# Near products in two terms, ten extra products ahead of two waits, and a later token scatter

## The chip, the cores and the metric

The kernel runs on one core of a Trainium2 chip. The metric is the time of one execution on the device in microseconds; the kernel before takes 2100.75 us, the median of 3 runs (2097.2 to 2100.86).

## The reference, cut to what matters

A transformer block on 16 sequences of 512 tokens with 256 features, in float32:

```python
qkv = x @ Wqkv + bqkv                       # 16 heads of 16 features
scores = stack([(q * shift(k, d)).sum(-1) for d in OFFSETS]) * scale + pos_bias   # d = 0..32, 48, 64, 96, 128, 192, 256, 384
alpha = softmax(scores)                     # over the 39 offsets, -inf where d > position
out = sum(alpha[d] * shift(v, d) for d in OFFSETS)
x = layernorm(x + (out * sigmoid(x @ Wgate + bgate)) @ Wout + bout)
logits = relu(x @ rw1 + rb1) @ rw2 + rb2    # 8 experts, the best 2 of each token, at most 1024 tokens an expert
x = layernorm(x + experts(x))               # relu(x @ ew1 + eb1) @ ew2 + eb2, weighted by the softmax of the two logits
```

## The kernel before

The kernel has three stages behind a short setup: `attention` (everything up to the first normalization, the router and the dispatch of tokens), `experts` and `combine`. The change touches `attention` alone. Float32 values are carried as a float16 high part plus a float16 low part, and a product is made of three terms, high by high, high by low and low by high.

`attention` works on one sequence (a batch) at a time, in a software pipeline. `run_iterations` writes the same plan for each engine: 20 iterations (-2 to 17), each of 16 slots; the middle ones, 2 to 13, are a hardware loop over two iterations at a time. `SLOTS_OF` (line 54) says which parts stand in which slot, `AHEAD` which batch a stage works on (the maxima on the next one, the output product on the one before, the ranking and the scatter on the one before that), and `LATER` by how many slots an engine takes a part later than TensorE (1 if it isn't named). Each engine takes its work strictly in that order. The tables `SCORES_AT`, `EXP_AT`, `SPLIT_AT`, `VALUES_AT` and `EVAC_AT` (lines 76 to 80) put the attention pairs into slots in the same way: a batch has 6 pairs k, 2 far ones (offsets that are multiples of 16) and 4 near ones (offsets 0 to 32, one for each tile of 128 tokens). A pair goes through `scores` (TensorE, banks `st`, lines 563 to 590), `weights` (ScalarE: the exponential twice, as float16 at line 789 and as float32 at line 790), `split_weights` (line 394: the float32 minus the float16, one half on VectorE and one on GpSimd), `values` (TensorE, line 622, banks `o[0]` and `o[1]`), and then either `evacuate_far` (ScalarE) or `merge` (VectorE, line 897: the near result plus the far one that came back through DRAM as `o_back`).

In `values` a near pair uses one `o` bank, `o[k % 2]`; for each of 4 blocks, 4 groups and 2 halves e it does three matmuls: high weights by the high values with the ones column (2 x 17 columns), high weights by low values (2 x 16), low weights by high values (2 x 17). All three add up in the same 17 columns.

The parts that matter beside these, in TensorE's order within an iteration: slot 5 `outp t` (transposes of the gated output, line 539), slot 6 `outp w` (its product with `wout`, line 546) and `maxp near0` (lines 678 to 688, which a reduction on VectorE, line 952, follows), slots 7 and 8 `near1` to `near3`, slots 9 and 10 `far0`, `far1` (lines 698 and 706), slot 10 `rout t`, slots 11 to 14 the router's hidden layer (`rout h0` to `h3`, line 546), slot 15 `feat x` (transposes of a new x), slots 0 and 1 the q and k projections. These parts share three PSUM banks `gp` in turn; by that order `outp w`'s first unit has the same bank as `outp t`'s first. ScalarE copies the transposed halves to `featT` (line 804). `rank s0` to `s3` issue on GpSimd two indirect DMAs each (line 1093), which scatter a batch's rows to their experts in DRAM (`disp`).

## Time and profile before

| | |
|---|---|
| median of 3 runs | 2100.75 us |
| the profiled execution | 2102.96 us |
| its span in the trace | 2101.2 us, mean granted TensorE clock 0.784 |
| busy in the span | TensorE 74%, VectorE 46%, ScalarE 43%, GpSimd 32% |
| costliest on TensorE | line 546 with `wr` 193.2 us, line 1385 173.0, line 1399 170.1, line 622 near 317 in all |

The attention stage fills about the first 1670 us, the experts run up to about 2055, and the rest is the last normalization. In the profile PE is TensorE, PEld its weight loads, DVE is VectorE, ACT ScalarE, POOL GpSimd, SP the queue that issues most DMAs. A bracket behind a row gives the idle time just before it and what ended that; "issue" there means that nothing the profile shows was waited for.

### The profile page before, as it was taken

Reading aid. Unit: us, or ns where it says so; the run is one execution under the profiler, and the core shown is the slowest. Engines: PE = TensorE matmul, PEld = TensorE weight load, DVE = VectorE, ACT = ScalarE, POOL = GpSimd, SP = SyncE. Lnnn points to the kernel's source line nnn. Section 1 sums busy time; section 2 is a strip of 40 time slices with the busy share of each in tenths; the row PEclk is TensorE's granted clock in tenths of the full one; section 3 lists DMA queues with packets and bytes.
Section 4 is the critical chain, followed back from the end, with each engine's and each line's share of the span. In section 5 each row is a group of like instructions: output and inputs, shape, how many; then the busy total and the mean of one; then the engine's idle time right before and its main releaser. Section 6 shows DMA issues by size and latency. Waiting matters only on the chain. (4 is left out here: it accounts for less than half of the span.)

```text
span 2101.2 us, 76212 instructions
## 1 busy us (share of the span) xinstructions
PE 1556.9 (74%) x33280; PEld 1045.3 (50%) x33280; DVE 962.6 (46%) x1925; ACT 907.8 (43%) x1544; POOL 674.4 (32%) x654
## 2 busy tenths in 40 slices
PE   0455786878777787878787777869676389999980
PEld 0234555545454455545455554545454247667660
DVE  4213354544445444545454454445455255554535
ACT  1232353534443352635254433526343366565626
POOL 4221333323241423333233415243332303232335
PEclk9665787868776786868687767768687689999995
DMA  3374524525251524334252514243330144444328
GB/s 82 63 203 135 107 77 92 103 76 114 74 117 49 114 64 96 82 74 98 63 114 64 115 49 103 64 87 74 66 86 3 45 134 102 98 90 111 66 31 325
DMA packets 220118, 194.80 MB, mean 93 GB/s; under 512 B 66847, under 2 KB 207151, under 8 KB 219648
## 3 DMA queue, kind: packets, MB, share of 16 engines
q1 hardware_dynamic: 204464, 175.11, 33.7%
q0 software_dynamic: 15360, 15.10, 4.5%
q8 instruction: 266, 4.36, 0.9%
q14 instruction: 28, 0.23, 0.0%
HBM read 98.07 MB, written 86.18 MB: 88 GB/s over the span
## 5 line engine op out<-in xcount | busy, mean ns | idle before, releaser
L394 POOL TENSOR_TENSOR p<-p 128x512 f16<-128x512 f32 x96 | 135.9, 1416 | 522.4 <-ACT p L790 522.2
L804 ACT COPY featT<-gp 128x1024 f16<-128x1024 f16 x96 | 93.4, 1032 | 430.4 <-PE gp L539 430.4
L394 DVE TENSOR_TENSOR p<-p 128x512 f16<-128x512 f32 x96 | 86.4, 900 | 293.4 <-ACT p L790 293.0
L546 PE MATMUL gp<-featT,wr 128*128 128x512 f16 x768 | 193.2, 410 | 19.8 <-DVE mT L945 13.6
L622 PE MATMUL o<-v_near,p 128*32 128x34 f16 (+1 forms) x6144 | 161.2, 185 | 33.9 <-issue 31.4
L1385 PE MATMUL up<-rowsT,w 128*128 128x512 f16 x768 | 173.0, 386 | 9.7 <-DVE w L1462 5.3
L622 PEld LDWEIGHTS o<-v_near,p 128*32 128x32 f16 x6144 | 153.7, 98 | 51.0 <-issue 47.9
L1347 POOL DMA_INDIRECT xln<-y,place x64 | 104.8, 1637 | 220.0 <-DVE y L1489 179.4
L789 ACT ACTIVATE p<-st 128x512 f16<-128x512 f32 x192 | 116.7, 608 | 126.1 <-PE st L590 109.4
L1399 PE MATMUL dn<-w,h 128*128 128x256 f16 x1536 | 170.1, 273 | 0.0
L1093 POOL DMA_INDIRECT disp<-y,sidx x128 | 137.9, 1078 | 65.2 <-issue 49.2
L1399 PEld LDWEIGHTS dn<-w,h 128*128 128x128 f16 x1536 | 149.7, 98 | 17.3
L952 DVE TENSOR_REDUCE m_near<-gp 128x8 f16<-128x512 f32 x128 | 82.1, 682 | 146.7 <-PE gp L688 93.8
L1446 ACT ACTIVATE h<-up,b 128x512 f16<-128x512 f32 x128 | 88.2, 689 | 131.1 <-PE up L1385 73.1
L546 PEld LDWEIGHTS gp<-featT,wr 128*128 128x128 f16 x768 | 76.0, 104 | 120.6 <-issue 35.3
L1385 PEld LDWEIGHTS up<-rowsT,w 128*128 128x128 f16 x768 | 76.0, 99 | 100.9 <-issue 11.4
L1080 POOL TENSOR_TENSOR x<-xin,x 128x1024 f16<-128x1024 f32 x16 | 34.0, 2125 | 280.2 <-ACT x L811 280.2
L1501 DVE TENSOR_TENSOR h<-h 128x512 f16<-128x512 f32 x128 | 88.6, 693 | 70.7 <-ACT h L1447 70.6
L546 PE MATMUL gp<-wout,featT 128*128 128x256 f16 x384 | 81.4, 405 | 49.8 <-ACT featT L804 49.8
L790 ACT ACTIVATE p<-st 128x512 f32<-128x512 f32 x192 | 118.1, 615 | 0.0
L546 PE MATMUL gp<-featT,wqk 128*128 128x512 f16 x384 | 112.9, 465 | 1.4 <-ACT featT L804 1.2
L874 ACT ACTIVATE hid<-gp,br 128x512 f16<-128x512 f32 x128 | 88.6, 692 | 55.6 <-PE gp L546 51.9
(173 smaller groups left out, 2953.7 us busy)
## 6 DMA issues: line engine op xcount, KB each, us to landing
qk_dram<-qk SPq DMA_DIRECT2D x64, 256.0 KB, 2.5
v_near<-vs SPq DMA_DIRECT2D x224, 66.0 KB
qs<-qk_dram SPq DMA_DIRECT2D x96, 128.0 KB, 4.6
ks<-qk_dram SPq DMA_DIRECT2D x96, 128.0 KB, 7.7
o_dram<-o_far SPq DMA_DIRECT2D x64, 136.0 KB, 5.9
o_back<-o_dram SPq DMA_DIRECT2D x16, 544.0 KB
v_dram<-vs SPq DMA_DIRECT2D x16, 528.0 KB, 3.3
v_far<-v_dram SPq DMA_DIRECT2D x64, 132.0 KB, 3.5
```

The source lines that it names most:

```text
L394: engine.tensor_tensor(p16[:, b, 1, :], p32[:, b, :], p16[:, b, 0, :], ALU.subtract).then_inc(is_split, 1)
L546: last = nc.tensor.matmul(dst, lhs(a, c), rhs(b, c), start=(k == 0), stop=(k == len(todo) - 1))
L622: last = nc.tensor.matmul(dst[quad, :, 2 * z + e, 0:cols.stop - cols.start], p16[:, 2 * (k % 2) + e, a, c:c + BLOCK], v[:, :, 2 * z + e, c ...
L789: nc.scalar.activation(p16[:, b, 0, :], bank[:, :], ACT.Exp)
L790: nc.scalar.activation(p32[:, b, :], bank[:, :], ACT.Exp).then_inc(exp_ready, 1)
L804: gp_done(nc.scalar.copy(featT[:, i, :, :].rearrange("f c t -> f (c t)"), bank[:, :].bitcast(F16)), n, stage, PART_OF_T[stage], i)
L874: nc.scalar.activation(hid16[:, 0, ht, :], bank[:, :], ACT.Relu, bias=br1[:, ht:ht + 1], scale=1.0 / WS)
L1093: nc.gpsimd.indirect_dma_start(out=disp[:, :], out_offset=bass.IndirectOffsetOnAxis(ap=sidx[:, t, k:k + 1], axis=0), in_=y16[n.par][:, t, ...
L1347: nc.gpsimd.indirect_dma_start(out=xln[:, :], out_offset=bass.IndirectOffsetOnAxis(ap=place[:, gr, t:t + 1], axis=0), in_=y[:, gr, t, :], ...
L1385: last = nc.tensor.matmul(up[h % 4][:, :], w1[e.par][:, a, c, P * h:P * (h + 1)], rowsT[:, gr, b, c, :], start=(k == 0), stop=(k == 5))
L1399: last = nc.tensor.matmul(dn[u][:, D * (t % 2):D * (t % 2 + 1)], h16[:, gr, a, h, P * t:P * (t + 1)], w2[e.par][:, b, h, :], start=(k == 0 ...
L1501: nc.vector.tensor_tensor(h16[:, gr, 1, h, :], h32[:, h % 2, :], h16[:, gr, 0, h, :], ALU.subtract).then_inc(h_lo, 1)
```

## The change

It has four parts. `rank s0, s1` move from slot 6 to slot 11 and `rank s2, s3` from slot 7 to slot 13 (GpSimd takes each one slot later). A near pair's three terms become two matmuls: high weights by high and low values together (2 x 33 columns), and low weights by high values (2 x 17) added onto the first 17; the results of the halves e go to the banks `o[0]` and `o[1]`, so that each near pair takes both and waits for the merge of the pair before. `merge` adds `o_back` to the first 17 columns of both halves and then, after a wait on its own semaphore, the other 16: four operations for one. And `keep_warm` writes ten 512-column products of router weights, which are overwritten by what follows, into the bank that the next part uses: ahead of the gated product in `outp w`, and ahead of the second far scores.

```diff
-    6: [("outp", "w"), ("maxp", "near0"), ("rank", "s0"), ("rank", "s1")],
-    7: [("rank", "s2"), ("rank", "s3"), ("outp", "y"), ("maxp", "near1")], 8: [("maxp", "near2"), ("maxp", "near3")],
+    6: [("outp", "w"), ("maxp", "near0")],
+    7: [("outp", "y"), ("maxp", "near1")], 8: [("maxp", "near2"), ("maxp", "near3")],
...
-    11: [("maxp", "t"), ("rout", "h0")],
-    12: [("rout", "h1"), ("gate0", "den0"), ("gate0", "inv0")], 13: [("rout", "h2")], 14: [("rout", "h3")], 15: [("feat", "x")],
+    11: [("maxp", "t"), ("rout", "h0"), ("rank", "s0"), ("rank", "s1")],
+    12: [("rout", "h1"), ("gate0", "den0"), ("gate0", "inv0")], 13: [("rout", "h2"), ("rank", "s2"), ("rank", "s3")], 14: [("rout", "h3")], 15: [("feat", "x")],
...
+            def keep_warm(bank, count):
+
+                for _ in range(count):
+                    nc.tensor.matmul(bank[:, :], wr1[:, 0, 0, 0:P], wr1[:, 0, 0, 0:512], start=True, stop=True)
...
+                banks = [st[(2 * k + e) % ST_BANKS] for e in range(2)]
+                if k == 1:
+                    wait(alone, exp_ready, n.at(2 * UNIT_PAIRS, 2 * k + 1 - ST_BANKS))
+                    keep_warm(banks[0], 10)
                 wait(alone, exp_ready, n.at(2 * UNIT_PAIRS, 2 * k + 2 - ST_BANKS))
...
-                elif k <= FAR_PAIRS + 1:
-                    alone.wait_ge(far_out, n.at(FAR_PAIRS, min(k, FAR_PAIRS)))
+                elif k <= FAR_PAIRS:
+                    alone.wait_ge(far_out, n.at(FAR_PAIRS, k))
                 else:
-                    alone.wait_ge(merged, n.at(TILES, k - FAR_PAIRS - 1))
+                    alone.wait_ge(merged, n.at(TILES, k - FAR_PAIRS))
...
+                            if not far:
+                                v = v_near[:, 4 * (k - FAR_PAIRS) + blk, :, 2 * z + e, :]
+                                dst = o[e][:, 0:PAIRS * VW].rearrange("q (u z c) -> q u z c", u=2, c=VW)[quad, :, z, :]
+                                nc.tensor.matmul(dst, p(0), v, start=True, stop=False, skip_group_check=True)
+                                last = nc.tensor.matmul(dst[:, :, 0:OW], p(1), v[:, :, 0:OW], start=False, stop=True, skip_group_check=True)
+                                continue
...
-                    drained(pe, n, "outp", "t", 0)
-                    drained(pe, n, "outp", "t", 1)
                     for u in range(2):
                         bank, is_full = unit(n, "outp", "w", u)
+                        if u == 0:
+                            keep_warm(bank, 10)
+                            drained(pe, n, "outp", "t", 0)
+                            drained(pe, n, "outp", "t", 1)
...
-                nc.vector.tensor_tensor(ob[:, i, :, :].rearrange("q h c -> q (h c)"), o[i % 2][:, 0:H * OW],
-                                        o_back[:, i, :, :].rearrange("q h c -> q (h c)"), ALU.add).then_inc(merged, 1)
+                of_e = lambda t, e: t[:, i, :, :].rearrange("q (u z e) c -> q e u z c", u=2, e=2)[:, e]
+                src = [o[e][:, 0:PAIRS * VW].rearrange("q (u z c) -> q u z c", u=2, c=VW) for e in range(2)]
+                for e in range(2):
+                    last = nc.vector.tensor_tensor(of_e(ob, e), src[e][:, :, :, 0:OW], of_e(o_back, e), ALU.add)
+                last.then_inc(merge_hi, 1)
+                dve.wait_ge(merge_hi, n.at(TILES, i + 1))
+                for e in range(2):
+                    num = of_e(ob, e)[:, :, :, 0:HD]
+                    last = nc.vector.tensor_tensor(num, src[e][:, :, :, OW:VW], num, ALU.add)
+                last.then_inc(merged, 1)
```

## Rows read from the trace of the kernel before

**Rows 1.** The page: busy time by engine, then TensorE's granted clock in 40 slices
```profile
PE 1556.9 (74%) x33280; PEld 1045.3 (50%) x33280; DVE 962.6 (46%) x1925; ACT 907.8 (43%) x1544; POOL 674.4 (32%) x654
...
PEclk9665787868776786868687767768687689999995
```

**Rows 2.** Timeline, TensorE, line 681: start us, us, instructions [idle before]; three of 16 batches
```profile
239.58 0.48 PE L681 MATMUL gp<-near_bias,sel_first 32*128 32x512 f16 x2
...
329.15 0.38 PE L681 MATMUL gp<-near_bias,sel_first 32*128 32x512 f16 x2
...
1482.93 0.38 PE L681 MATMUL gp<-near_bias,sel_first 32*128 32x512 f16 x2
```

**Rows 3.** Operations by tile, `disp`, GpSimd: ns min/median/max, first and last start us
```profile
L1093 POOL DMA_INDIRECT disp<-y,sidx x128: 966/976/2010, 335.2 to 1669.2; - x128
```

**Rows 4.** Timeline, TensorE, from near1 to far0 in an iteration with a scatter
```profile
719.85 0.39 PE L678 MATMUL gp<-near_bias,sel 32*128 32x512 f16 x2
...
723.70 0.27 PE L688 MATMUL gp<-ks,qs 16*32 16x64 f16 x5 [0.46 <-issue]
...
733.07 0.61 PE L678 MATMUL gp<-near_bias,sel 32*128 32x512 f16 x2 [3.64 <-DVE m_near L952]
...
735.23 0.39 PE L698 MATMUL gp<-far_bias,sel 32*128 32x256 f16 x2 [0.88 <-DVE m_near L952]
```

**Rows 5.** Timeline, TensorE, near1 and far0 in iteration 1, which has no scatter
```profile
245.13 0.39 PE L678 MATMUL gp<-near_bias,sel 32*128 32x512 f16 x2
...
254.41 0.40 PE L698 MATMUL gp<-far_bias,sel 32*128 32x256 f16 x2 [0.90 <-DVE m_near L952]
```

**Rows 6.** Timeline, GpSimd, first and last of the scatter's eight DMAs
```profile
720.24 1.11 POOL L1093 DMA_INDIRECT disp<-y,sidx  x1 [0.91 <-issue]
...
730.10 0.98 POOL L1093 DMA_INDIRECT disp<-y,sidx  x1 [0.30 <-issue]
```

**Rows 7.** Timeline, VectorE: two reductions of near2, and the merge of pair 4
```profile
732.23 1.29 DVE L952 TENSOR_REDUCE m_near<-gp 128x8 f16<-128x512 f32 x2 [6.32 <-remote]
...
761.17 0.43 DVE L897 TENSOR_TENSOR ob<-o,o_back 128x272 f32<-128x272 f32 x1
```

**Rows 8.** Timeline, GpSimd, its subtractions for pairs 4 and 5
```profile
752.15 1.61 POOL L394 TENSOR_TENSOR p<-p 128x512 f16<-128x512 f32 x1
761.68 1.54 POOL L394 TENSOR_TENSOR p<-p 128x512 f16<-128x512 f32 x1 [7.92 <-ACT p L790]
```

**Rows 9.** Timeline, TensorE, the parts that the change touches or meets in this iteration
```profile
708.94 5.30 PE L546 MATMUL gp<-wout,featT 128*128 128x256 f16 x24 [3.32 <-ACT featT L804]
...
749.05 4.08 PE L546 MATMUL gp<-featT,wr 128*128 128x512 f16 x12 [0.26 <-issue]
...
760.45 5.35 PE L546 MATMUL gp<-featT,wr 128*128 128x512 f16 x24
765.73 2.33 PE L622 MATMUL o<-v_near,p 128*32 128x34 f16 x96
...
775.59 0.40 PE L563 MATMUL st<-sel,far_bias 64*128 64x256 f16 x2 [2.25 <-ACT p L790]
...
783.72 2.54 PE L622 MATMUL o<-v_far,p 128*32 128x68 f16 x96
```

**Rows 10.** Timeline, TensorE, wide products of the expert stage
```profile
1856.59 10.52 PE L1385 MATMUL up<-rowsT,w 128*128 128x512 f16 x48
```

**Rows 11.** Timeline, GpSimd, the indirect DMA beside them
```profile
1859.63 1.56 POOL L1347 DMA_INDIRECT xln<-y,place  x1 [11.45 <-DVE y L1489]
```

**Rows 12.** Timeline, ScalarE, its copies of the transposed gated output
```profile
706.91 1.98 ACT L804 COPY featT<-gp 128x1024 f16<-128x1024 f16 x2
```

**Rows 13.** Stretches: from:to us, length, busy by engine (instructions), granted TensorE clock, DMA share, GB/s
```profile
708.90:714.20 5.30, 5.26 (x26) 3.40 (x28) 3.20 (x13) 0.00 (x0) 1.14 (x1) 0.50 0.76 148
...
732.00:751.00 19.00, 15.26 (x527) 11.21 (x528) 5.67 (x10) 3.98 (x6) 1.18 (x2) 0.59 0.02 3
...
775.50:779.00 3.50, 3.41 (x135) 2.13 (x136) 3.46 (x3) 0.94 (x2) 1.20 (x1) 0.50 0.43 94
```

## What the change will do to the time

> **What bounds the kernel now.** I read the shares of busy time on the page first: TensorE is busy for 74% of the span, no other engine for half of it [rows 1]. The 40 slices then show where its clock is held back: in the attention loop, slices 2 to 31, it is granted at 5 to 8 tenths, while the expert stage behind it has 9s [rows 1]. So the loop over 16 batches is TensorE's: its instructions stand in one order for all batches, and what it waits for, or does at half clock, is time. How long one batch takes is read from the first near-maximum product (line 681), which stands once in each iteration: between the iterations that start it at 329.15 and at 1482.93 lie twelve, 96.15 us each; but the iteration from 239.58 to 329.15 took 89.57 us [rows 2]. The two differ in the one thing that the diff moves: the first scatter of tokens (line 1093) comes at 335.2 [rows 3], so iteration 1 has none, and iterations 2 to 14 have one beside the near-maximum products.
>
> The timeline of TensorE shows what it does there. With a scatter, the products from near1 on (719.85) reach far0 at 735.23, 15.4 us later; without one the same work goes from 245.13 to 254.41, 9.3 us [rows 4, 5]. Inside the scatter (GpSimd's row at 720.24; its last DMA at 730.10) [rows 6] TensorE issues three to five products and stands 0.46 us, with no releaser but "issue" [rows 4], and it then waits 3.64 us for VectorE's reduction [rows 4], which itself had stood 6.32 us for something the profile calls "remote" [rows 7]. Neither is there in iteration 1. The chain of what ended last is no help for this: it lies in the last normalization.
>
> **The change part by part.** The profiled execution took 2102.96 us, its span 2101.2 with 1.8 around it, and the median of three runs is 2100.75. I make the sum against 2102.96 and take the 2.2 off at the end.
>
> *The scatter moves* from GpSimd's places at slots 7 and 8 to slots 12 and 14 of an iteration: eight indirect DMAs, the last starting 9.86 us after the first [rows 6], so 1.4 from one to the next; four and four make two stretches of 5.2. What it gives back is 15.4 - 9.3 = 6.1 us by the stretch, 96.15 - 89.57 = 6.6 by the whole iteration. 13 iterations by 6.3 make **-82 us** (-79 to -86). With the gaps gone, what is late next in the stretch is the chain through VectorE, GpSimd and ScalarE that makes y, and the wait for each reduction; both are inside the 9.3 already.
>
> What it costs in its new place: GpSimd reaches slot 12 after its subtraction for pair 4 (752.15, 1.61 long) and slot 14 after pair 5 (761.68, 1.54) [rows 8]. The four DMAs would run from about 753.8 to 758.9 and from 763.2 to 768.4. GpSimd has nothing due between (its next subtraction is that of the first far pair, whose exponential TensorE itself still waits for at 775.59 [rows 9], by when GpSimd is free), and the semaphores that the scatter waits for are long up. Its buffers are wanted again in the next iteration's slot 6, over 35 us later. TensorE does wide products there: the second stretch lies beside line 546 (760.45, 24 of them) and then the 96 products of pair 5 (765.73) [rows 9]. In the expert stage an indirect DMA of 1.56 us at 1859.63, with three behind it, leaves the 48 wide products from 1856.59 on whole: 10.52 us, 0.219 each, no gap [rows 10, 11]. So wide products aren't held. Narrow ones are, three to five in 0.73 us (the row's 0.27 and the 0.46 ahead of it) [rows 4]: pair 5 would overlap the second stretch by at most 2.7 us. SP's queue issues the maxima, the copies of v and the next x beside these stretches; none is wanted before the next first far scores. Below: 0. Above: the whole 6.6 comes back. I take 1.5 a batch, near the lower end because that is the case of the expert row and the stretch is cut in two, over 14 iterations: **+21 us**.
>
> That TensorE should suffer at all is against the Trainium skill: "SBUF — State Buffer", section "Who interferes with whom", says that only the port pair shared by VectorE and GpSimd contends and that TensorE and ScalarE wait for nobody. By that rule the 0.46 us gaps are none of the scatter's and would stay; the case is the first rival below, and the trace with and without a scatter speaks against it.
>
> *The near product of values (line 622)* goes from three matmuls of 34, 32 and 34 columns to two of 66 and 34: 96 a pair become 64, with as many weight loads. 96 near ones take 2.33 us, 24.3 ns each; 96 far ones, of 68 and 64 columns, take 2.54, so 26.5 each [rows 9]. Doubling the columns costs 2 ns: it is their number that counts. 64 take 32 x 26.5 + 32 x 24.3 ns = 1.63 us, a gain of 0.70. Pairs 3, 4 and 5 of a batch lie in TensorE's dense stretches (3 x 16 x 0.70 = 34 us); pair 2 lies ahead of near1, whose reduction waits for y anyway, and counts a quarter: **-37 us**. Bounds: 0, were it the columns that count (they stay 100), and -45 with pair 2 in full.
>
> *The merges on VectorE (line 897)*: one addition of 272 elements, 0.43 us [rows 7], becomes two of 136, a wait for their end, and two of 128. A reduction of 512 elements takes 0.65 (two in 1.29) [rows 7], so an element costs 0.9 ns and an operation 0.2 beside that: 528 elements in four operations are 1.3 us, +0.85 each, and each result now uses both o banks, so that pair k waits for the merge of k - 1 and not of k - 2. The tightest is pair 5: merge 4 begins at 761.17 and would end at 762.5, pair 5 starts at 765.73 [rows 7, 9]. In VectorE's queue behind a merge stand the hidden layer's subtractions, which ScalarE needs three products later. 0 us; if the cover is gone (VectorE held by the scatter), 0.85 x 16 = 14.
>
> *Ten products ahead of the gated product.* They go into bank 0, which the first gated transpose also used, so they start only when ScalarE's first copy is done: two copies, 1.98 us from 706.91 [rows 12], hence 707.9. The old wait ended at 708.94, so just 1.0 of its 3.32 us is left to fill. A 512-column product takes 0.219 at full clock [rows 10], about twice that at half: ten end between 710.1 and 712.2. What they could give is the clock: the 24 products after the wait took 5.3 us [rows 9] at a granted clock of 0.50 [rows 13] and would take half that at full clock. Old end 714.2; new end between 710.1 + 2.65 = 712.8 and 712.2 + 5.3 = 717.5. The clock fell with an idle stretch of 3.3 us and 2.3 of these stay, so it still falls; it may rise sooner. I take the middle, +1.0 a batch.
>
> *Ten ahead of the second far scores*: TensorE ended its transposes at 773.34 and waited 2.25 us for ScalarE [rows 9]. The products fill that at full clock (2.19) and overshoot by 2 at half. The 3.5 us after the wait were at 0.50 [rows 13], worth 1.7. Between -1.8 and +2.0; middle -0.6, since a fuller stretch brings the clock back sooner and the wait is nearly as long as they are. Both together (1.0 - 0.6) x 16 = **+6 us**, bounds -51 and +85, each only if all 32 fall to one side.
>
> **Sum**: -82 + 21 - 37 + 6 = -92. 2102.96 - 92 = 2011; less 2.2, **2009 us**.
>
> **Rivals.** *The gaps belong to the narrow products, not to the scatter*: then moving it gives nothing and costs nothing, -37 + 6 = -31, **2070 us**. For it: the gaps sit only on narrow products. Against: iteration 1 has these and not the gaps [rows 5]. 8%. The Trainium skill's rule named above is this case.
>
> *The clock comes back in the near stage.* Granted was 0.59 from 732 to 751, with the narrow products dense for much of it [rows 13]. If the shorter stage lets it rise earlier, the transposes and the first hidden product (749.05, 12 in 4.08 us, where 24 of them take 5.35 later) [rows 9] save about 2.6 us a batch: 34 more, **1975 us**. Against: iteration 1's stage has VectorE's waits too. 10%.
>
> *The hold moves along, and gets worse (slower).* VectorE's reduction at 732.23 started 12.0 us after the scatter's first DMA [rows 6, 7]. If each half holds VectorE in slots 12 to 15, the merge of pair 4 comes late, pair 5 must wait for it (a wait that the change adds), the subtractions keep ScalarE from draining, and the wide products run out of banks. At 4 us of holding twice and 3.6 of narrow products in pair 5 and the next far scores, 11.6 a batch: 14 x 11.6 = 162 in place of 21, with the rest -113: **2150 us**. It decides from (82 + 37 - 6)/14 = 8.1 us a batch on. For it: the remote wait has no named cause [rows 7]. Against: each half is half as long and meets wide products. 7%.
>
> *The products cost at half clock throughout*: +85 in place of +6, the rest holding: **2088 us**. Against: 24 wide products at 760.45 took 5.35 us [rows 9], full speed, so the clock does return under dense work. 5%.
>
> **Numbers.** Forecast 70%, gaps stay 8, clock back 10, hold moves 7, half clock 5. The range must leave out 2 in 10 at most: from 1975 (clock back) to 2072, which takes in the case that the gaps stay and most of the upper end of the new place (6.6 a batch, 2009 + 71 = 2080). Faster by over 0.2% 0.89, within 0.2% 0.03, slower 0.08; 0.2%, 4 us, is about what a measurement of this kernel can tell.
>
> **What would show it.** Right: line 681's starts 90 us apart in all iterations; no 0.46 us gaps from near1 to far0; 4096 near matmuls in 64s of 1.6 us; gated product starting 1 to 3 us later after its wait, scores' transposes followed by ten products and no wait. Wrong: gaps still in near1 (first rival); VectorE waiting for "remote" after slot 12, or "values" waiting for line 897's successors (third). The step I trust least is the price of the scatter's new place, then the clock after the ten products.

## The result: 30 us faster, a third of what was forecast

The changed kernel takes 2071.01 us (median of 4 runs, 2067.58 to 2081.45), the kernel before 2100.81 beside it (4 runs, 2097.2 to 2103.67): ratio 0.9867, 95% interval 0.9829 to 0.9906. Forecast was 2009. The profiled execution took 2071.61 us with a span of 2069.9 and a mean granted TensorE clock of 0.827 (0.784 before). The first busy line and the clock line of its page, which answer to [rows 1]:

```profile
PE 1571.6 (76%) x31552; PEld 1021.9 (49%) x31552; DVE 992.3 (48%) x2117; ACT 905.3 (44%) x1544; POOL 703.0 (34%) x654
...
PEclk9676788879787887979787887978787699999995
```

TensorE is busy 15 us longer (320 extra products, less the shorter near ones) and its clock line has more 8s and 9s in the attention loop; the span still lost only 31 us. Line 693 is the old line 681; its starts, as in [rows 2]:

```profile
327.17 0.38 PE L693 MATMUL gp<-near_bias,sel_first 32*128 32x512 f16 x2
...
1450.06 0.38 PE L693 MATMUL gp<-near_bias,sel_first 32*128 32x512 f16 x2
```

Twelve iterations take 93.57 us each, against 96.15. I use this measure for all kernels below ("an iteration"): the start of the fourth such product to that of the sixteenth, by 12. It is read from the one profiled execution of each kernel.

**What went as forecast.** The stretch of [rows 4], from near1 to far0 (lines 690 and 710 now), in the changed kernel, and then the group of the near-maximum products over the whole run, before and after (operation, count, ns min/median/max; under it the idle time before them, us and times):

```profile
707.67 0.39 PE L690 MATMUL gp<-near_bias,sel 32*128 32x512 f16 x2
...
709.06 0.61 PE L700 MATMUL gp<-ks,qs 16*32 16x64 f16 x56 [0.85 <-issue]
712.93 0.61 PE L690 MATMUL gp<-near_bias,sel 32*128 32x512 f16 x2 [3.25 <-DVE m_near L974]
...
717.76 0.39 PE L710 MATMUL gp<-far_bias,sel 32*128 32x256 f16 x2 [0.88 <-DVE m_near L974]
```

```profile
L688 PE MATMUL gp<-ks,qs x4096: 171/227/238, 85.4 to 1502.3; 16*32 16x64 f16 x185, 16*32 16x32 f16 x11
...
  issue: 148.7, 260
```

```profile
L700 PE MATMUL gp<-ks,qs x4096: 171/226/238, 83.6 to 1464.0; 16*32 16x64 f16 x185, 16*32 16x32 f16 x11
...
  issue: 39.7, 81
```

near1 starts at 707.67, far0 at 717.76: 10.1 us, against 15.4. The products still stand once for 0.85 us, not every few products, and over the run their "issue" time fell from 148.7 us in 260 places to 39.7 in 81. So the gaps left with the scatter, and VectorE's waits for "remote" too (its waits over the run: us, times, longest), before and after:

```profile
DVE m_near L952 <- remote: 53.0, 9, 8.4
```

```profile
DVE ob L914 <- remote: 8.3, 2, 4.2
```

**What did not.** In the gated product's place (TensorE's timeline and two stretches; columns as in [rows 13]):

```profile
695.29 4.45 PE L545 MATMUL gp<-wr 128*128 128x512 f16 x10 [2.40 <-ACT featT L818]
699.53 3.17 PE L551 MATMUL gp<-wout,featT 128*128 128x256 f16 x24
```

```profile
695.30:699.70 4.40, 4.40 (x11) 1.64 (x12) 3.37 (x12) 0.85 (x1) 2.00 (x1) 0.50 1.15 127
699.80:702.60 2.80, 2.80 (x24) 2.26 (x22) 0.69 (x1) 0.00 (x0) 0.00 (x0) 0.91 0.90 212
```

The ten products run at 0.50 of the clock and take 4.45 us; the 24 behind them then run at 0.91 and take 3.17 instead of 5.30 [rows 9]. Over the run, ten by sixteen each:

```profile
L545 PE MATMUL st<-wr x160: 376/380/634, 110.0 to 1509.4; 128*128 128x512 f16 x160
...
L545 PE MATMUL gp<-wr x160: 379/634/634, 234.9 to 1593.6; 128*128 128x512 f16 x160
```

The median of the ones ahead of the gated product (`gp`) is 634 ns, that of the ones ahead of the second far scores (`st`) 380: the first mostly meet half clock, the second mostly full.

In the scatter's new place (GpSimd, VectorE, TensorE in the same iteration):

```profile
736.01 4.17 POOL L1115 DMA_INDIRECT disp<-y,sidx  x1 [0.17 <-issue]
```

```profile
737.12 1.48 DVE L1006 TENSOR_TENSOR hid<-rows,hid 128x512 f16<-128x512 f32 x2
738.52 0.67 DVE L952 SCALAR_TENSOR_TENSOR og<-eg,ob 128x512 f32<-128x512 f32 x1
```

```profile
737.54 4.45 PE L551 MATMUL gp<-featT,wr 128*128 128x512 f16 x12 [2.07 <-DVE mT L967]
...
743.95 0.19 PE L629 MATMUL o<-v_near,p 128*32 128x66 f16 x1 [0.50 <-issue]
...
744.93 0.18 PE L630 MATMUL o<-v_near,p 128*32 128x34 f16 x1 [0.73 <-issue]
```

The first DMA takes 4.17 us instead of 1.1, TensorE's second hidden product waits 2.07 us for VectorE and takes 4.45 us, and the value products of pair 4 behind it stand several times (0.50, 0.73), so that they reach from 742 to 745.4.

### The profile page after: what moved, and what is told of

Read it like the earlier page. It is cut to its first block and busy times, and to the rows that moved or that the text cites. A ratio compares the mean times of both kernels' runs of the same rounds, so it can differ in the third digit from the quotient of the medians.

```text
span 2069.9 us, 72972 instructions
## 1 busy us (share of the span) xinstructions
PE 1571.6 (76%) x31552; PEld 1021.9 (49%) x31552; DVE 992.3 (48%) x2117; ACT 905.3 (44%) x1544; POOL 703.0 (34%) x654
## 5 line engine op out<-in xcount | busy, mean ns | idle before, releaser
L394 POOL TENSOR_TENSOR p<-p 128x512 f16<-128x512 f32 x96 | 129.6, 1350 | 465.7 <-ACT p L804 465.7
L394 DVE TENSOR_TENSOR p<-p 128x512 f16<-128x512 f32 x96 | 94.9, 988 | 310.6 <-ACT p L804 303.5
L551 PE MATMUL gp<-featT,wr 128*128 128x512 f16 x768 | 204.5, 426 | 26.7 <-DVE mT L967 19.5
L1115 POOL DMA_INDIRECT disp<-y,sidx x128 | 172.6, 1349 | 52.9 <-issue 37.9
L629 PE MATMUL o<-v_near,p 128*32 128x66 f16 x2048 | 132.3, 202 | 43.4 <-issue 31.6
L629 PEld LDWEIGHTS o<-v_near,p 128*32 128x32 f16 x2048 | 118.0, 105 | 67.4 <-issue 66.7
L630 PE MATMUL o<-v_near,p 128*32 128x34 f16 x2048 | 130.8, 192 | 12.5 <-issue 12.4
L630 PEld LDWEIGHTS o<-v_near,p 128*32 128x32 f16 x2048 | 118.5, 98 | 9.9 <-issue 9.3
L867 ACT ACTIVATE y<-y,nmr,rstd 128x256 f32<-128x256 f32 x64 | 33.2, 588 | 180.4 <-POOL nmr L1098 180.4
```

The lines of the kernel that those rows point to most:

```text
L394: engine.tensor_tensor(p16[:, b, 1, :], p32[:, b, :], p16[:, b, 0, :], ALU.subtract).then_inc(is_split, 1)
L551: last = nc.tensor.matmul(dst, lhs(a, c), rhs(b, c), start=(k == 0), stop=(k == len(todo) - 1))
L629: nc.tensor.matmul(dst, p(0), v, start=True, stop=False, skip_group_check=True)
L630: last = nc.tensor.matmul(dst[:, :, 0:OW], p(1), v[:, :, 0:OW], start=False, stop=True, skip_group_check=True)
L1115: nc.gpsimd.indirect_dma_start(out=disp[:, :], out_offset=bass.IndirectOffsetOnAxis(ap=sidx[:, t, k:k + 1], axis=0), in_=y16[n.par][:, t, ...
```

## The experiments

Kernels with the same number for the kernel before ran on one chip, beside it. There turned out to be two sorts of chip: the result and e1 to e8 stand on chips where the kernel before takes about 2100 us (the first sort), e9 to e18 on three others where it takes about 2024 (the second sort). No chip was measured on two occasions, so whether it is the chip itself or something else about the occasion isn't shown; "sort of chip" stands for either.

| kernel | kernel before beside it | median | ratio (95%) | iteration |
|---|---|---|---|---|
| before / the change (result) | 2100.81 | 2071.01 | 0.9867 (0.9829 to 0.9906) | 96.15 / 93.57 |
| e1 no products | 2109.29 | 2030.10 | 0.9628 (0.9581 to 0.9675) | 91.05 |
| e2 no far products | 2109.29 | 2066.34 | 0.9814 (0.9767 to 0.9861) | 92.71 |
| e3 no gated products | 2109.29 | 2047.71 | 0.9716 (0.9670 to 0.9762) | 92.15 |
| e4 scatter moved alone | 2109.29 | 2076.60 | 0.9863 (0.9816 to 0.9910) | 93.62 |
| e5 terms alone | 2096.78 | 2061.49 | 0.9816 (0.9786 to 0.9845) | 93.32 |
| e6 no scatter | 2096.78 | 1966.72 | 0.9368 (0.9336 to 0.9400) | 87.36 |
| e7 far products before branch | 2096.78 | 2045.33 | 0.9733 (0.9691 to 0.9776) | 91.81 |
| e8 first half in q and k | 2096.78 | 2025.72 | 0.9655 (0.9626 to 0.9684) | 90.23 |
| e9 scatter in one place | 2022.41 | 1984.18 | 0.9804 (0.9780 to 0.9828) | 87.64 |
| e10 plain DMAs | 2022.41 | 1976.62 | 0.9767 (0.9736 to 0.9798) | 87.03 |
| e11 four gated products | 2022.41 | 1990.41 | 0.9828 (0.9795 to 0.9862) | 88.51 |
| e12 one part a slot | 2022.41 | 1977.60 | 0.9768 (0.9750 to 0.9787) | 87.33 |
| e13 before again | 2026.19 | 2028.34 | 1.0006 (0.9983 to 1.0029) | 90.23 |
| e14 change again | 2026.19 | 2023.55 | 0.9995 (0.9972 to 1.0018) | 91.08 |
| e15 no products again | 2026.19 | 1976.65 | 0.9768 (0.9727 to 0.9808) | 87.09 |
| e16 one part a slot again | 2026.19 | 1978.17 | 0.9778 (0.9738 to 0.9818) | 87.04 |
| e17 plain DMAs again | 2023.91 | 1981.77 | 0.9805 (0.9771 to 0.9838) | 87.35 |
| e18 one place again | 2023.91 | 1983.89 | 0.9812 (0.9782 to 0.9842) | 87.36 |

### The parts one by one: e1 to e4

e1 is the change without both sets of ten, e2 keeps the gated ones, e3 the far ones, e4 is the kernel before with nothing but the new places of the scatter:

```diff
 # e1 and e2
-                if k == 1:
-                    wait(alone, exp_ready, n.at(2 * UNIT_PAIRS, 2 * k + 1 - ST_BANKS))
-                    keep_warm(banks[0], 10)
 # e1 and e3
-                            keep_warm(bank, 10)
 # e4, in the kernel before
-    6: [("outp", "w"), ("maxp", "near0"), ("rank", "s0"), ("rank", "s1")],
-    7: [("rank", "s2"), ("rank", "s3"), ("outp", "y"), ("maxp", "near1")],
+    6: [("outp", "w"), ("maxp", "near0")],
+    7: [("outp", "y"), ("maxp", "near1")],
...
+    11: [("maxp", "t"), ("rout", "h0"), ("rank", "s0"), ("rank", "s1")],
...
+    13: [("rout", "h2"), ("rank", "s2"), ("rank", "s3")],
```

> The change without its twenty products an iteration; the terms, the merge and the moved scatter stay. From the two traces I read, start to start and as means over iterations 4 to 13: the stretch from the transposes of x to the values of the first far pair grew by 1.4 us, that from the ranking's product to the end of the gated product by 0.6. Theory (they cost more than the clock returns): taking them away gives 2.0 x 15 = 30 us back, 2071 - 30 = 2041. Rival (the prediction's sizes, +1.0 and -0.6 an iteration): 2071 - 6 = 2065, no difference to speak of.

> The change without the ten products ahead of the second far scores, those ahead of the gated product stay. Theory (TensorE's sequencer spends 4.6 us in the loop's branch in every second iteration, and only then comes to the ten products, which therefore fill nothing): 2071 - 1.4 x 15 = 2050. Rival of the prediction (they gain 0.6 an iteration): 2071 + 9 = 2080. The branch's row should fall back from 4.6 us to near the 3.9 of before or stay, and the following wait should again be one for ScalarE's exponential.

> The change without the ten products ahead of the gated product, those ahead of the second far scores stay. Theory: 2071 - 0.6 x 15 = 2062. By the prediction's +1.0: 2056. Were the products worth their price here: 2071 or more. The gated product's 24 matmuls, 3.2 us in the change, should take 5.3 again.

> The kernel before with the scatter moved and nothing else. Theory (the move gives 5.7 us an iteration in the near stage and takes 4.7 in the hidden layer): 13 x 5.7 - 14 x 4.7 = 8 us, 2093. The prediction (82 given, 21 taken): 2040. Rival (the held place is worse without the shorter near products): over 2101.

**Measured**: without any product 2030.1 us, with the gated ones 2066.3, with the far ones 2047.7. By the ratios both together cost 0.9867 - 0.9628 = 0.0239, some 50 us, where the sum had 6 (the intervals of two such ratios leave about 13 us either way); the gated ones alone 36 us (2066.3 - 2030.1), the far ones 18. The moved scatter alone gives 0.0137, 29 us. What I expected of these runs was off in size each time: 30 us for both sets; 21 for taking the far ones out of the change (measured 0.9867 - 0.9814, 11 us) and 9 for taking the gated ones out (0.9867 - 0.9716, 32 us); and 8 for the moved scatter.

Where the far products' time goes is in TensorE's timeline of the change: first an iteration that ends in the hardware loop's branch, then one that doesn't:

```profile
660.63 1.07 PE L539 MATMUL gp<-ident,x 128*128 128x128 f16 x16
665.88 4.13 PE L545 MATMUL st<-wr 128*128 128x512 f16 x10 [4.18 <-ACT p L804]
```

```profile
755.34 1.57 PE L539 MATMUL gp<-ident,x 128*128 128x128 f16 x13
...
757.64 2.67 PE L545 MATMUL st<-wr 128*128 128x512 f16 x10
```

In the second the ten start at once behind the transposes and take 2.67 us, near the 2.19 of the forecast. In the first, TensorE stands 4.18 us before them and they then take 4.13 us. The profile puts the wait down to ScalarE, but in this iteration the branch instruction runs from 660.87 to 665.62, and the ten start at 665.88. The branch (line 189, ns min/median/max), before and after:

```profile
L189 PEldq COMPARE_BRANCH  x6: 82/3858/4057, 481.1 to 1446.8; - x6
```

```profile
L189 PEldq COMPARE_BRANCH  x6: 83/4566/5042, 473.6 to 1413.5; - x6
```

Before, the 3.86 us of the branch lay almost wholly under the wait for ScalarE's exponential: from the transposes of x to the scores behind them it took 4.2 to 4.5 us with a branch and 3.7 to 4.0 without. The change's products stand behind the branch in the order, so in these iterations they don't fill the wait but follow it: 8.8 to 9.7 us with a branch, 4.7 to 6.8 without. The Trainium skill says of this, in "Runtime: NRT & Kernel Launch", section "Instruction fetch mechanics", that a taken branch whose target isn't among the pages at hand forces a fetch before execution goes on, and that straight code mostly hides its fetches; it gives no time. The rows give 3.9 to 4.6 us for the whole branch and don't show what it waits for. With one set alone it stays at 3.4 to 4.1 us (e2, e3), so the 4.6 belongs to both sets together.

### Terms, scatter, and the products ahead of the branch: e5 to e8

e5 is the change with the scatter in its old place and no products. e6 is e1 with the scatter's DMAs and the waits on them left out. e7 is e3 with the ten far products at the end of slot 15. e8 is e1 with the scatter's first half in slot 1 of the next iteration (and the hardware loop from iteration 4 on):

```diff
 # e6
-                        nc.gpsimd.indirect_dma_start(
-                            out=disp[:, :], ...).then_inc(scattered, 16)
 # e7, behind the transposes of x at the end of slot 15
+                m = n.shift(-1)
+                if m.in_range():
+                    wait(alone, exp_ready, m.at(2 * UNIT_PAIRS))
+                    keep_warm(st[2], 10)
 # e8
-    11: [("maxp", "t"), ("rout", "h0"), ("rank", "s0"), ("rank", "s1")],
+    11: [("maxp", "t"), ("rout", "h0")],
+    0: [("scat", "s0"), ("scat", "s1"), ("proj", "qk0"), ("gate", "den1"), ("gate", "inv1")],
```

> The kernel before with the near products in two terms and the four-part merge, scatter in its old place, no extra products. Theory and prediction agree on the mechanism (64 narrow products for 96): -37 us by the prediction's term, 2101 - 37 = 2064 or a ratio of 0.982; by the rows of the change, 0.84 and 0.97 us at pairs 2 and 3, somewhat more. Rival (columns count, or the merge's 0.85 us and the wait for it come to the front): ratio of 1.00.

> The two-term kernel without the extra products and with no scatter at all: the eight indirect DMAs and the waits for them are left out, so the expert stage works on cleared rows, and one wait is added there between a group's two halves. It prices the scatter wherever it stands. Theory (the new place costs some 4.7 us an iteration): pair 4's values fall from 3.7 to 1.6 us, and the iteration from 91.2 to about 86.5; 2030 - 66 = 1964. The prediction's 1.5 an iteration: 2030 - 21 = 2009.

> No products ahead of the gated product; the other ten are issued at the end of slot 15, right behind the transposes of x and ahead of the loop's branch, into the same bank. Theory (the sequencer's 4.6 us in the branch kept them from filling the wait): now they run while it is in the branch, nothing is added in the iterations that end in one, and against the kernel without products (ratio 0.963) the first q and k products run at full clock: ratio 0.958 to 0.965, that is at least the 1.7 us an iteration of the other place back. Rival (the products are simply work on a path that has no room): as in the other place, ratio 0.972.

> The two-term kernel without extra products, and the first four of the eight DMAs issued one iteration later, in slot 1 on GpSimd ahead of its q and k subtractions (for that four iterations instead of two are written out ahead of the loop, and one behind it); the last four stay in slot 14. Theory A (the price of the new place is its first half: the first DMA takes 4.2 us of GpSimd there and pair 4's 64 narrow products stretch to 3.7 us): pair 4 falls to 1.6, the iteration loses 3 to 4 us against 91.2, ratio 0.942. Theory B (the narrow products are held wherever the scatter stands, in slots 1 and 2 as well): ratio near 0.963.

**Measured**: the terms alone 0.9816, some 39 us (forecast 37). From e5 to e6 the scatter in its old place costs 2061.49 - 1966.72 = 95 us, and an iteration is 5.96 longer; the near-maximum products of both:

```profile
L697 PE MATMUL gp<-ks,qs x4096: 171/227/238, 85.2 to 1467.3; 16*32 16x64 f16 x185, 16*32 16x32 f16 x11
...
  issue: 151.0, 268
```

```profile
L697 PE MATMUL gp<-ks,qs x4096: 171/227/238, 84.9 to 1392.1; 16*32 16x64 f16 x185, 16*32 16x32 f16 x11
...
  issue: 41.0, 82
```

From e6 to e1 it costs 0.9628 - 0.9368 = 0.0260 in its new place, 55 us, 3.69 an iteration; the forecast had 21. Some 14 us of the 95 and 13 of the 55 are no hold: between TensorE's last product of the attention stage and its first `up` product of the experts lie 27.9 us in e5, 26.8 in e1 and 13.6 in e6, because the last batch's scatter stands there in every kernel but e6. So the old place itself cost about 81 us and the new one about 42.

Where an iteration of e1 spends its 3.69 us more than one of e6 (means of twelve iterations, from the start of a part to the start of the next): value products of pair 4 3.70 against 1.63, of pair 5 2.22 against 1.63, the second hidden product 3.34 against 2.97, and the third and fourth, 24 wide products right behind pair 4, 6.24 against 5.28; the other parts together take 0.3 less. These 24 are not held, there is no gap in them; they run partly at half clock. One such place in the change, on the timeline and as a stretch (columns as in [rows 13]):

```profile
1025.68 8.16 PE L551 MATMUL gp<-featT,wr 128*128 128x512 f16 x24
```

```profile
1025.60:1033.80 8.20, 8.20 (x26) 3.01 (x26) 3.58 (x8) 3.67 (x6) 4.88 (x5) 0.65 0.64 151
```

They take more than 5.5 us in six of twelve iterations of the change and in eight of e1, wherever pair 4 is held (e2, e3, e4 and e7 too), and 5.35 in all twelve of the kernel before, e5, e6, e8 and every kernel of the second sort. So products ahead of which TensorE was made to stand pay as well, through the clock.

e8 takes 0.9655 against e1's 0.9628: the value products of pair 4 are back at their undisturbed time, but the scores of pairs 0 and 1, which now stand beside the first half, grow by 1.8 and 1.3 us. On this chip the hold is paid wherever narrow products stand beside the scatter.

e7 came out where its rival had it (0.972, work on a path that has no room): 0.9733, 91.81 an iteration, against e3's 92.15 and e1's 91.05. So the place behind the branch isn't the whole price of the far ten. An iteration without a branch shows why:

```profile
933.10 1.07 PE L539 MATMUL gp<-ident,x 128*128 128x128 f16 x16
934.01 2.32 PE L545 MATMUL st<-wr 128*128 128x512 f16 x10
...
941.02 5.34 PE L551 MATMUL gp<-featT,wqk 128*128 128x512 f16 x24 [2.19 <-issue]
```

The ten run at full clock (2.32 us) where TensorE used to wait, and then TensorE stands 2.19 us for "issue" before the q and k product. There are seven such gaps in e7 and seven in e3, none in the loop of e1, but only one in the change. That the wait for ScalarE had also covered a fetch of instructions is my reading; the row shows only that the gap is there once the wait is filled.

### Places and forms of the scatter, on a chip that holds nothing: e9 to e12

```diff
 # e9, from e1: all four parts behind rout h2
-    11: [("maxp", "t"), ("rout", "h0"), ("rank", "s0"), ("rank", "s1")],
+    11: [("maxp", "t"), ("rout", "h0")],
-    ... 13: [("rout", "h2"), ("rank", "s2"), ("rank", "s3")],
+    ... 13: [("rout", "h2"), ("rank", "s0"), ("rank", "s1"), ("rank", "s2"), ("rank", "s3")],
 # e10, from e1
-                        nc.gpsimd.indirect_dma_start(out=disp[:, :], ...)
+                        nc.gpsimd.dma_start(disp[bass.ds(n.at(N, t * P + half * k), half), :],
+                                            y16[n.par][half * k:half * (k + 1), t, :].bitcast(U32)).then_inc(scattered, 16)
 # e11, from e1
+                            keep_warm(bank, 4)
 # e12, from e1: s0 in slot 11, s1 in 12, s2 in 13, s3 in 14
```

> Two near terms, no extra products, and all eight scatter DMAs of a batch behind pair 5's subtraction (GpSimd's slot 14) instead of four in slot 12 and four in slot 14. Theory A, the scatter's price in its new place is that of holding the narrow value products of pair 4 and of VectorE's transposes-copy and subtraction holding the first DMA: then the value products of pair 4 take 1.6 us instead of 3.7, the first DMA no longer takes over 4 us, and only the later stretch grows, by about 1; an iteration takes about 90.0 us against 91.2 with the halves apart, 2012 us, ratio 0.955. Theory B, the scatter holds whatever narrow products it meets, some 3.4 us a batch wherever it stands in the second half: an iteration stays at 91.2, 2030 us, ratio 0.963, and the scores of pairs 0 and 1 of the next batch take the 2 to 4 us more.

> Two near terms, no extra products, scatter in its new place, but each of the eight indirect DMAs is replaced by a plain one from GpSimd that moves 64 rows to fixed places (the routed placement is left out, so the experts work on other tokens; about as many bytes move). It asks what of the scatter holds TensorE: if it is GpSimd's work for the indirect form, the value products of pair 4 fall from 3.7 to about 1.7 us, an iteration from 91.2 to about 88 (as without any scatter, 87.7), some 1972 us, ratio 0.94. If it is the rows that move, or any DMA that GpSimd issues, pair 4 stays near 3.7 and the iteration near 91, ratio 0.96.

> The change without the ten products ahead of the second far scores, and with four instead of ten ahead of the gated product. Theory A, what the ten cost is that they run at half clock, 0.45 us each, past the end of the wait for ScalarE's copies: four take 1.8 us, end within the wait of 3.8, and the wait side grows by at most 0.3 instead of 3.1; the gated product stays near 5.4 or falls a little; the iteration is 90.7 to 91.2, ratio 0.960 to 0.963. Theory B, the price is one of each product (0.19 us each net, as 1.9 for ten): an iteration 91.9, 2040 us, ratio 0.967.

> Two near terms, no extra products, and one scatter part (two DMAs) in each of four slots in a row (TensorE's slots 11 to 14) instead of two parts in two slots. Theory A, the hold grows with the DMAs that stand in a row before a narrow phase: pair 4's value products meet two DMAs, 2.7 us instead of 3.7, the rest is spread under wide products; an iteration 90.4 us, ratio 0.957. Theory B, every DMA holds what it meets by the same 0.4 us: no change against the halves (91.2, ratio 0.963).

**Measured**: the kernel before took 2022.41 us here, so ratios can't be set against those of e1 to e8. That was the discovery: e11 has its scatter where e1 has it, and the value products of pair 4 took 1.63 us, not 3.70. The places differ little (e9 0.9804, e12 0.9768, e10 0.9767), and e9 and e10 could not decide what they were made for, as there was no hold to remove. e11 decides more. In it:

```profile
674.88 1.89 PE L545 MATMUL gp<-wr 128*128 128x512 f16 x4 [2.40 <-ACT featT L815]
676.56 3.46 PE L551 MATMUL gp<-wout,featT 128*128 128x256 f16 x24
```

The four start when ScalarE's first copy is done, as the ten do, run at half clock, end after the second copy, and bring the gated product to 3.46 us (4.3 as a mean of twelve iterations, 5.3 without products). At this place the sum is next to nothing: from the ranking's second set of products (`chosen`) to what follows the gated one it takes 8.87 us, in e12 beside it 9.04 and in e15 8.86; with all ten (e14) 9.69, 0.8 more, near the 1.0 of the forecast. Yet the iteration is 88.51 against e12's 87.33, and the kernel is at 0.9828 against 0.9768, 12 us: nearer theory B (one price a product, 8 us) than theory A, but not by its mechanism, since the price is not paid where the products stand. Some of it is in the iterations with a branch: there the transposes of x are cut by an "issue" gap of 0.4 to 1.2 us in all five of e11 and in none of e12, and from them to the scores it takes 4.69 us against 3.95.

One thing e10 shows beside this. Its first four plain DMAs stand where the indirect ones stood, beside the same VectorE operations, and take 0.5 to 0.6 us each:

```profile
708.30 2.21 POOL L1112 DMA_DIRECT2D disp<-y  x4
```

As far as these runs go, the 4.2 us of the first DMA come with the indirect form alone.

### The same kernels on one chip of the second sort: e13 to e16, and e17, e18

e13 is the kernel before and e14 the change, unedited; e15 is e1, e16 is e12, e17 is e10 and e18 is e9.

> The kernel before, as it is, for its trace on the chip of this call: the last four kernels ran on a chip on which the kernel before took 2022 us instead of 2100. Theory A, on that chip GpSimd's scatter DMAs don't hold TensorE's narrow products, and on the earlier chips they do: if this call's chip is such a one (kernel before near 2022), the near block 1 and 2 phases take about 4.4 and 2.1 us instead of 7.2 and 3.7, and an iteration takes about 90.5 us; if it is like the earlier ones (2100), they take 7.2 and 3.7 again, 96.4 an iteration. Theory B, the chip is faster in something else (transfers, clock): then the 78 us are spread over all phases and near 1 stays near 7 us.

> The change as it is. Theory A: on a chip where the kernel before takes 2022 us, the scatter's move is worth nothing, the two terms give back 2.5 us an iteration and the twenty products take 2.5, so the change is within 10 us of the kernel before, ratio 0.995 to 1.005; on a chip where before takes 2100 us, ratio 0.986 as in the result. Theory B (the chip is faster in everything alike): ratio 0.986 on either.

> The change without both sets of ten products. Theory A: on a chip where before takes 2022 us, only the two terms' 2.5 us an iteration are left, 1982 us, ratio 0.980; on a 2100 us chip 0.963 as before. Theory B: 0.963 on either.

> Two near terms, no extra products, one scatter part in each of TensorE's slots 11 to 14. On a chip where before takes 2022 us: as the halves (ratio 0.977 to 0.980), since nothing is held. On a 2100 us chip: theory A, the hold grows with the DMAs that stand in a row before a narrow phase, an iteration 90.4 us, ratio 0.957; theory B, every DMA holds what it meets alike, 91.2, ratio 0.963.

> Two near terms, no extra products, scatter in its new place with eight plain DMAs of 64 rows from GpSimd for the eight indirect ones (the routed placement is left out, so the experts work on other tokens). It says something only on a chip where the kernel before takes 2100 us: if the hold is of the indirect form, the value products of pair 4 take 1.7 us and the ratio is 0.94; if any DMA issued by GpSimd, or the rows moved, holds them, they take 3.7 us and the ratio is 0.963. On a chip where before takes 2025 us: ratio 0.977, pair 4 at 1.64, as in the first such call.

> Two near terms, no extra products, all eight scatter DMAs behind pair 5's subtraction (GpSimd's slot 14). On a chip where before takes 2100 us: if a hold falls on whatever narrow products it meets, pair 4 is back at 1.64 us and the scores of pairs 0 and 1 of the next batch and the value products of pair 5 take 2 to 4 us more, an iteration of 91.2 and ratio 0.963; if wide products and ScalarE's waits there cover it, 89 an iteration and ratio 0.945. On a chip where before takes 2025 us: 0.980, as in the first such call.

**Measured**: theory A. e13 takes 90.23 us an iteration (90.5 expected), e14 0.9995, e15 0.9768 (0.980 expected). The kernel before, with its scatter in the old place, on such a chip, TensorE from near1 to far0, GpSimd beside it, and the near-maximum products of the run:

```profile
696.75 0.39 PE L678 MATMUL gp<-near_bias,sel 32*128 32x512 f16 x2
...
697.80 0.52 PE L688 MATMUL gp<-ks,qs 16*32 16x64 f16 x38 [0.45 <-issue]
701.38 0.60 PE L678 MATMUL gp<-near_bias,sel 32*128 32x512 f16 x2 [3.06 <-DVE m_near L952]
...
705.94 0.40 PE L698 MATMUL gp<-far_bias,sel 32*128 32x256 f16 x2 [1.12 <-DVE m_near L952]
```

```profile
697.14 1.11 POOL L1093 DMA_INDIRECT disp<-y,sidx  x1 [0.91 <-issue]
...
699.83 1.74 POOL L1093 DMA_INDIRECT disp<-y,sidx  x1 [0.30 <-issue]
```

```profile
L688 PE MATMUL gp<-ks,qs x4096: 171/228/238, 83.0 to 1425.1; 16*32 16x64 f16 x185, 16*32 16x32 f16 x11
...
  issue: 48.6, 81
```

9.2 us from near1 to far0, with the scatter inside, its first DMA as long as in [rows 6]: it was 15.4 on the other sort of chip [rows 4] and 9.3 there in an iteration without a scatter [rows 5]. The "issue" time is 48.6 us, not 148.7. The span of the kernel before is 75.3 us shorter than on the first sort (2025.9 against 2101.2), and 71.1 of that lie in the twelve iterations, 5.93 each: what leaving the scatter out gave on the first sort (5.96). So the hold makes nearly the whole difference between the two sorts. With nothing held there is next to nothing for the move to give back. The old place is not quite free, though: the eight DMAs stand in GpSimd's order ahead of its subtraction for pair 3, and the value products wait for that in 11 of the 12 iterations, 1.26 us an iteration, which e15 doesn't have:

```profile
709.96 2.22 PE L622 MATMUL o<-v_near,p 128*32 128x34 f16 x79 [1.46 <-POOL p L394]
```

In the new place nothing is held either; the low-part value products of the change on the first sort of chip, and on this one:

```profile
L630 PE MATMUL o<-v_near,p x2048: 177/180/222, 151.8 to 1572.7; 128*32 128x34 f16 x187
...
  issue: 21.7, 42
```

```profile
L630 PE MATMUL o<-v_near,p x2048: 177/181/223, 152.7 to 1534.3; 128*32 128x34 f16 x187
...
  issue: 1.8, 2
```

What is left is the terms' gain, perhaps with a few us of that wait, and the products' price: 0.9768 without the products (47 us gained, where the terms alone gave 39 on the first sort) and 0.9995 with them (0.9995 - 0.9768 = 0.0227, 46 us lost again). The change that gains 30 us on one sort of chip gains nothing that can be measured on the other.

e14 and e15 also show a part of the products' price that lies elsewhere. The router's second hidden product (12 products behind the wait for `mT`), first without, then with the products:

```profile
714.80:717.40 2.60, 2.60 (x15) 1.08 (x14) 2.57 (x4) 1.27 (x2) 2.45 (x1) 1.00 0.03 9
```

```profile
729.20:733.60 4.40, 4.40 (x15) 1.50 (x16) 4.37 (x4) 1.26 (x2) 3.79 (x3) 0.61 0.30 101
```

1.00 of the clock without and 0.61 with. Of twelve iterations it took the long way (4.3 to 4.5 us in place of 2.8) in one of e15 and in seven of e14. On this sort of chip, then, part of the full clock that the products buy is missing later. On the first sort both e1 and the change have five such iterations, so there it explains nothing, and why the clock is lower is not shown.

The rest can be read from what TensorE does in the twelve iterations (its rows and the idle time before them, summed between the fourth and the sixteenth start, by 12). From e15 to e14 an iteration grows by 3.99 us: TensorE is busy 3.65 longer, although its granted clock rises from 0.775 to 0.814; it waits 2.37 less for ScalarE, as was meant, but 0.97 more for VectorE, and it stands 1.97 more for "issue" (5.50 against 3.53). From e1 to the change it is 2.52: 3.26, 1.89 less, 0.84 and 0.65. So the filled waits come back in part as other waits; what the added "issue" time is isn't shown.

e16, e17 and e18 came on this sort of chip as well, and repeat e12, e10 and e9 (0.9778, 0.9805, 0.9812). Whether plain DMAs hold TensorE on a chip of the first sort, and what the one place behind rout h2 would bring there, stays open.

## Why the prediction came out too low

By its own steps, in its own order, with the ratios taken on some 2100 us:

| term | forecast | measured (kernels) |
|---|---|---|
| scatter leaves its old place | -82 | -95 (e5 to e6), of which 81 in that place; near 0 on the second sort of chip (e13) |
| its new place | +21 | +55 (e6 to e1), of which 42 in that place; no hold on the second sort (e15) |
| near products, two terms | -37 | -39 (e5) |
| merges | 0 | in that -39 |
| the twenty products | +6 | +50 (e1 to the change); +46 on the second sort (e15 to e14) |
| together | -92 | -29; the result has -30 |

**What bounds the kernel, and the removal of the scatter: right in mechanism, and in size for this sort of chip.** The gaps and the remote wait of VectorE belonged to the scatter: 53.0 us of VectorE's "remote" waits before, none in e6, and none in e13 either. The 6.3 us an iteration was 5.96, and the total of 82 was 81, once the 14 us between the stages, which e6 leaves out and no move of the scatter gives back, are taken from the 95. The evidence that bore the forecast was the pair of stretches [rows 4, 5], and it held. The other half of it did not: iteration 1 is shorter than the later ones, but in e13, where no scatter holds anything, it takes 92 us and the later ones 90.23, so its total says nothing of the scatter, though 6.6 happened to be near.

**The near products: right** (the working's own parts, 33.6 and 2.8, make 36, not 37). Number and not columns decides: from the first of them to the next part, 64 take 1.63 us in pairs 4 and 5 of e15, and the 96 of the kernel before took 2.27, so 0.64 less for a forecast 0.70. **The merges: right.** Four operations take 1.0 us (0.51 and 0.49 in the timeline of the change), and over the whole run the high-part value products waited once for a merge.

**The new place: mechanism foreseen, size wrong by 34 us** (13 of them the stretch between the stages, which cancels against the 95; 21 the place itself). The failing step is "TensorE does wide products there". I checked the second stretch (763.2 to 768.4) against pair 5, and not the first: it was put at 753.8 to 758.9, just ahead of the narrow value products of pair 4, which in that iteration run right ahead of line 546's product at 760.45 [rows 9], from 758.2. The first DMA then took 4.17 us and not 1.1, so that the stretch slid 3 us to the right, onto them: 3.70 us in place of 1.63. And "wide products aren't held" was true without being enough: the 24 behind pair 4 lost 0.96 us an iteration to the clock. How the slide came the rows suggest: VectorE's last operation with two inputs from SBUF (`og`) ends at 739.19 and the DMA at 740.18; a DMA takes 0.97 to 1.1, as if this one had started only then. (It was issued at 736.01, beside `mT`, which has one input from SBUF and one from PSUM, so what held it up to the next operation at 737.12 isn't shown.) In e15 the same pair is at 716.26 and 717.25, and in e9, behind pair 5, none of the eight takes over 1.5 us. This agrees with the Trainium skill, "SBUF — State Buffer", section "Who interferes with whom", which has VectorE operations with two SBUF inputs contend with GpSimd instructions that read SBUF, and infers that making descriptors isn't held by them: the indirect DMAs read their indices there and were held, the plain ones of e10 were not. I had cited that section for TensorE and not asked which VectorE work stands in the new place. What it also says, that TensorE waits for nobody, doesn't hold as it stands on the chips of the first sort (148.7 us of gaps, 41.0 without a scatter), by whatever path, and does on the others (48.6 with it).

**The products: wrong, and the largest miss, 44 us.** *Ahead of the gated product* the local step held: half clock, 4.45 us, the 24 behind them nearly at full clock, +1.0 an iteration (e1 to the change) and +0.8 (e15 to e14) against +1.0. *Ahead of the far scores* the step that fails is "The products fill that at full clock and overshoot by 2 at half". The wait that I read, 2.25 us in an iteration without a branch [rows 9], stood for every second iteration only. In the others, the products queue behind a branch of 4.4 to 5.0 us and come after it; from the transposes of x to the first scores they cost +2.7 us an iteration (6.72 against 4.02), with 1.3 given back by the q and k product (5.70 against 6.99): +1.4, where the forecast had -0.6. *Beside both* there is what the forecast had nothing for: on the second sort of chip another 1.7 us an iteration, the router's second product at half clock in seven iterations of twelve instead of one (+0.8) and small losses elsewhere, partly as "issue" time, that I can't name. On the first sort the two places make 2.4 of the 2.52 us in the profiled executions, but the medians differ by 50 us, 3.1 a batch. The gated ten alone cost 36 us in e2, more than twice the 16 that their place shows, so most of that price stays open. Both together were given bounds of -51 to +85, and +50 lies within them; taking the middle, +6, was the error. The rival "half clock throughout" had +85 at 5% and was a little nearer to the price, though only the gated set runs so.

**The rivals.** "The gaps belong to the narrow products" gave 2070 us, and 2071 was measured; it is refuted all the same, by the fall from 148.7 to 39.7 us: the sum met it by chance. "The clock comes back in the near stage" didn't show: near1 to far0 still took 10.1 us, all of the gain on it being the gaps. "The hold moves along" is half true, at 3.7 us an iteration and not 8.1, and it has a piece that I had named (narrow products in slots 12 to 15) and two that I hadn't (VectorE holds GpSimd, not the other way round, and the clock is late for the wide products behind). The sign that I had named, VectorE waiting for "remote" ahead of the merges, shows twice (8.3 us). That a chip may show no hold at all was not among the cases, and no row of a trace from one chip could have told.

**Versions.** The best on either sort of chip leaves out both sets of ten: e1 and e8 at 0.9628 and 0.9655 on the first, e15 and e12 at 0.9768 on the second, against 0.9867 and 0.9995 for the change.

## What to carry to other kernels

A wait may cover more than the thing it is named for: before filling it with extra work, look in every kind of iteration for a branch, a fetch or a clock step that lies under it, and price the filler as if it came behind all of them. When work is moved, lay its new interval over every engine's timeline there, with its start late by what may hold it (here VectorE's two-input operations ahead of GpSimd's first DMA), and price both ends of the interval. And a gain that rests on "issue" gaps without a named releaser should be measured on more than one chip: here it was 6 us an iteration on some and none on others.

## What the hardware showed beyond that

- The same program with the same DMAs has its narrow TensorE products held on some chips (kernel before: 2089 to 2113 us) and not on others (2016 to 2035 us), with the same granted clock (0.78 to 0.80). With the scatter left out, or on the other sort, an iteration is 5.9 to 6.0 us shorter. Wide products are held on neither, but those right behind held ones ran partly at a granted 0.50 (up to 8.5 us for 24 in place of 5.35). What of the scatter holds them, and why only on some chips, is open.
- TensorE's loop branch takes 3.9 us before and 4.6 us with both sets of extra products, every second iteration; a wait for another engine hid nearly all of it until that wait was filled.
- An indirect DMA of 1.0 us on GpSimd took 4.2 us (at most 4.3) beside VectorE operations with two inputs from SBUF, on both sorts of chip; a plain DMA in its place took 0.6.
- Ten products of 512 columns at a granted 0.50 brought the 24 products behind them to 0.91; four did nearly as much in the iteration shown (3.46 us against 3.17, from 5.3) and half as much in the mean (4.3 against 3.0), and in both cases the whole kernel became slower.
